# Nearest neighbours and sixteen residual layers on one core: low parts by adding DMAs, and a reordered first stage

## The reference

```python
sq = jnp.sum(xyz * xyz, axis=1)
d2 = sq[:, :, None] + sq[:, None, :] - 2.0 * jnp.einsum('bdn,bdm->bnm', xyz, xyz)
_, idx = jax.lax.top_k(-d2, 8)
...
for i in range(4):                          # and the whole again: 8 layers
    shortcut = points
    p = leaky_relu(points)                  # slope 0.01
    g = group_point(p, idx_t)               # p of the 8 nearest points
    c = jnp.einsum('oi,bin->bon', w[i], p)
    gn = jnp.einsum('oi,bikn->bokn', w[i], g)
    points = (c + gn.sum(axis=2)) / 9.0 + shortcut
```

## Time and profile before

| | |
|---|---|
| median of three runs | 345.85 us |
| the profiled execution's own time | 345.5 us |
| its span in the trace | 343.4 us |
| PE busy | 322.1 us (94%) |
| DVE busy | 276.8 us (81%) |
| ACT busy | 164.3 us (48%) |
| POOL busy | 87.8 us (26%) |
| DMA, hardware queue | 18.36 MB, 16.8% of 16 engines |

### The profile page before, as it was taken

One profiled execution on the slowest core, in us unless ns is written; L12 is line 12 of the kernel. 1 busy time (PEld: TensorE's weight loads), 2 busy tenths in 40 slices (PEclk: granted clock), 3 DMA queues, 4 the chain that ended last, 5 costly groups with the idle time before them and its releaser, 6 DMA issues.

```text
span 343.4 us, 5071 instructions
## 1 busy us (share of the span) xinstructions
PE 322.1 (94%) x2024; PEld 293.3 (85%) x2024; DVE 276.8 (81%) x350; ACT 164.3 (48%) x246; POOL 87.8 (26%) x76
## 2 busy tenths in 40 slices
PE   4999799969989869999999999999999999999996
PEld 4999799969979758887888988898898889889884
DVE  3998999999999594888867777977877796787773
ACT  4536445533726714355844655436265643626510
POOL 2000000000006302333724523514252351425200
PEclk9999999989999989999999999999999999999999
DMA  7945534514700000000000000000000000000023
GB/s 242 326 147 168 153 98 143 180 61 124 240 22 1 0 2 0 2 0 0 2 0 2 0 3 2 0 2 0 2 0 2 0 0 2 0 2 0 37 88 122
DMA packets 7311, 18.68 MB, mean 54 GB/s; under 512 B 628, under 2 KB 1908, under 8 KB 7288
## 3 DMA queue, kind: packets, MB, share of 16 engines
q1 hardware_dynamic: 7288, 18.36, 16.8%
HBM read 16.26 MB, written 2.10 MB: 53 GB/s over the span
## 4 chain that ended last, share of the span: by engine, by line
PE 46%; DVE 5%; ACT 1%; issue 1%; DVEq 0%
PE wide L424 26%; PE wide L413 7%; PE wide L400 6%; PE wide L402 6%; DVE r_mixed L658 1%; DVE y_rest L726 1%; DVE y_lo L730 1%; DVE state L738 1%; ACT y_hi L572 1%; ACT relu L564 0%; PE wide L386 0%; DVEq L713 0%; ACT r_high L567 0%; DVEq L729 0%
## 5 line engine op out<-in xcount | busy, mean ns | idle before, releaser
L281 POOL TENSOR_TENSOR r_low<-relu,r_high 128x512 fp32r<-128x512 f32 x64 | 85.5, 1351 | 234.2 <-ACT r_high L567 234.2
L424 PE MATMUL wide<-adj,y_hi 128*128 128x512 f32 (+1 forms) x260 | 101.8, 393 | 0.8 <-DVE state L738 0.8
L424 PE MATMUL wide<-adj,y_lo 128*128 128x512 f32 (+1 forms) x260 | 101.7, 393 | 0.0
L726 DVE TENSOR_TENSOR y_rest<-wide,y_hi 128x1024 f32<-128x1024 f32 x32 | 39.2, 1224 | 43.3 <-ACT y_hi L572 43.3
L400 PE MATMUL wide<-w_high,r_high 128*128 128x256 f32 x256 | 63.6, 286 | 0.4 <-DVE y_rest L726 0.4
L402 PE MATMUL wide<-w_low,r_low 128*128 128x256 f32 x256 | 63.2, 284 | 0.0
L572 ACT CAST y_hi<-wide 128x1024 fp32r<-128x1024 f32 x32 | 32.3, 1008 | 62.4 <-PE wide L402 62.4
L564 ACT ACTIVATE relu<-state 128x512 f32<-128x512 f32 x64 | 40.2, 629 | 39.2 <-DVE state L738 30.4
L424 PEld LDWEIGHTS wide<-adj,y_hi 128*128 128x128 f32 x260 | 48.9, 188 | 11.2 <-DVE state L738 1.2
L424 PEld LDWEIGHTS wide<-adj,y_lo 128*128 128x128 f32 x260 | 49.0, 188 | 10.2
L400 PEld LDWEIGHTS wide<-w_high,r_high 128*128 128x128 f32 x256 | 49.4, 193 | 2.1 <-issue 0.8
(11 more groups left out here) (59 smaller groups left out, 289.5 us busy)
## 6 DMA issues: line engine op xcount, KB each, us to landing
raw<-in_ctx_dram SPq DMA_DIRECT2D x23, 512.0 KB, 4.2
state<-in_x_dram SPq DMA_DIRECT2D x4, 512.0 KB, 6.4
out_dram<-state SPq DMA_DIRECT2D x3, 512.0 KB, 2.8
w_raw<-in_fside_BxSxS_dram SPq DMA_DIRECT2D x1, 1024.0 KB, 10.8
rest_raw<-in_ctx_dram SPq DMA_DIRECT2D x4, 130.0 KB
raw<-in_ctx_dram SPq DMA_DIRECT2D x2, 256.0 KB, 3.2
out_dram<-state SPq DMA_DIRECT2D x1, 256.0 KB, 2.0
out_dram<-state SPq DMA_DIRECT2D x2, 128.0 KB, 1.7
```

The costliest lines, as they stand in the source:

```text
L281: nc.gpsimd.tensor_tensor(r_low[:, n % 3, h, :], relu[:, h, :], r_high[:, n % 3, h, :].bitcast(fp32), ALU.subtract).then_inc(r_low_ready, 1)
L424: mm = nc.tensor.matmul(bank[to][:, cols], part[:, s % 2, q, h * P:(h + 1) * P], adj[:, b, q, cols], start=(q == 0 and part is y_hi), stop ...
L726: nc.vector.tensor_tensor(y_rest[:, :, :], wide[MAIN][:, :].rearrange("p (q o) -> p q o", q=NB), y_hi[:, s % 2, :, :].bitcast(fp32), ALU.s ...
```

## The change

Six edits go together. (1) `BY_DMA` is (1, 3, 5): in batches 1 to 3 the low parts of units 1, 3 and 5 are no longer computed on VectorE. ACT multiplies the loaded words by -`LEAN` in place, and a DMA issued by GpSimd reads the same words from DRAM once more and adds them. (2) A load waits for the main products of the unit one batch earlier (`main_used`) and for its mixed part (`g_mixed_ready`); VectorE's `points_mixed` now waits for `unit_used` itself. (3) The row of half squares is one fp32 product of `ones` and `half_diag`; the split into two fp32r parts is gone. (4) On VectorE `distances` comes after unit 1's mixed and unit 2's low part, the other units are dispersed between the searches, and the four `weights` stand behind unit 0 of batch 1. ACT's order is moved accordingly. (5) `turn_neighbours(2)`, `copy_adj(2)` and the third relu come after the first `y_step`. (6) `ENTER` is 9, and what is done for batch 3 between the steps comes one step later.

```diff
-    BY_DMA = ()
+    BY_DMA = (1, 3, 5)
...
-        ENTER = 8
+        ENTER = 9
...
                     if k < PAIRS:
-                        sp.wait_ge(unit_used, (b - 1) * PAIRS + k + 1)
+                        sp.wait_ge(main_used, (b - 1) * PAIRS + k + 1)
                     else:
-                        sp.wait_ge(mixed_summed, b * NB)
+                        sp.wait_ge(main_summed, b * NB)
+                    sp.wait_ge(g_mixed_ready[k], b)
...
-                pe.wait_ge(diag_split, b + 1)
-                nc.tensor.matmul(bank[SQ_BANK][:, :], ones[:, :], diag_hi[:, :], start=True, stop=False)
-                nc.tensor.matmul(bank[SQ_BANK][:, :], ones[:, :], diag_lo[:, :],
-                                 start=False, stop=True).then_inc(sq_row_ready, 1)
+                pe.wait_ge(diag_ready, b * NB + NB)
+                nc.tensor.matmul(bank[SQ_BANK][:, :], ones[:, :], half_diag[:, :], start=True, stop=True)\
+                    .then_inc(sq_row_ready, 1)
...
                 mixed_products(b, 4)
-                if b == B - 1:
-                    turn_neighbours(B - 2)
...
                 if s == 0:
+                    turn_neighbours(B - 2)
+                if s == 1:
                     square_row(B - 1)
...
-                if s == 1:
+                if s == 2:
                     turn_distances(B - 1)
...
+            points_parts(1, 0)
+            points_parts(1, 1)
             weights_high(0)
             weights_high(1)
-            points_parts(1, 0)
-            points_parts(1, 1)
+            points_parts(1, 2)
+            points_parts(1, 3)
             weights_high(2)
             weights_high(3)
-            points_parts(1, 2)
             copy_main(0)
-            points_parts(1, 3)
+            points_parts(1, 4)
             for b in range(1, B):
-                points_parts(b, 4)
+                points_parts(b, 5)
+                points_parts(b, 6)
                 if b >= 2:
                     copy_adj(b - 2)
-                points_parts(b, 5)
-                points_parts(b, 6)
+                copy_low(b - 1)
...
+                if b > 0 and k < PAIRS:
+                    dve.wait_ge(unit_used, (b - 1) * PAIRS + k + 1)
+                elif b > 0:
+                    dve.wait_ge(mixed_summed, b * NB)
...
                 diagonals(b - 1)
-                split_diagonal(b - 1)
-                for k in (2, 3, 5):
-                    points_low(b, k)
-                    points_mixed(b, k)
+                points_low(b, 1)
+                points_mixed(b, 1)
+                points_low(b, 2)
                 distances(b - 1)
...
+                points_mixed(b, 2)
+                points_low(b, 3)
+                points_low(b, 4)
+                points_mixed(b, 3)
+                points_low(b, 5)
                 neighbours(b - 1, 0)
                 neighbours(b - 1, 1)
+                points_low(b, 6)
+                points_mixed(b, 6)
+                points_mixed(b, 4)
+                neighbours(b - 1, 2)
+                neighbours(b - 1, 3)
+                points_mixed(b, 5)
...
-                if s == 0:
+                if s == 1:
                     distances(B - 1)
                     relu_mixed(2)
...
-                if 2 <= s < 2 + NB:
-                    neighbours(B - 1, s - 2)
-                if s == 6:
+                if 3 <= s < 3 + NB:
+                    neighbours(B - 1, s - 3)
+                if s == 7:
                     add_selves(B - 1)
```

More of the change, by code:

```diff
@@ L100, in knn_blocks_kernel @@
         half_diag = sb("half_diag", [P, N], fp32)
-        diag_hi = sb("diag_hi", [P, N], fp32r)
-        diag_lo = sb("diag_lo", [P, N], fp32r)
         half_sq = sb("half_sq", [P, NB], fp32)
@@ L108, in knn_blocks_kernel @@
         eyes = sb("eyes", [P, NB, P], bf16)
-        ones = sb("ones", [P, P], fp32r)
+        ones = sb("ones", [P, P], fp32)
         w_raw = sb("w_raw", [P, BLOCKS, CH, C], fp32)
@@ L176, in knn_blocks_kernel @@
         unit_in = [sem(f"unit_in_{k}") for k in range(UNITS)]
+        main_used = sem("main_used")
         unit_used = sem("unit_used")
@@ L193, in knn_blocks_kernel @@
         diag_ready = sem("diag_ready")
-        diag_hi_ready = sem("diag_hi_ready")
-        diag_split = sem("diag_split")
         sq_row_ready = sem("sq_row_ready")
@@ L282, in relu_low @@
                                             ALU.subtract).then_inc(r_low_ready, 1)
-            pool.memset(ones[:, :].bitcast(fp32), 1.0).then_inc(consts_ready, 1)
+            pool.memset(ones[:, :], 1.0).then_inc(consts_ready, 1)
             pool.memset(ident[:, :], 0.0).then_inc(eye_zeroed, 1)
@@ L328, in main_products @@
                             mm.then_inc(main_summed, 1)
+                if k < PAIRS:
+                    mm.then_inc(main_used, 1)
             def mixed_products(b, k):
@@ L595, in _ @@
                         nc.scalar.mul(w_low[:, l, :, :], w_raw[:, l, :, :], SHIFT).then_inc(w_ready, 1)
-                copy_low(b - 1)
                 if b < B - 1:
@@ L601, in _ @@
                     points_parts(b + 1, 2)
+                    points_parts(b + 1, 3)
                     copy_main(b)
                     neighbour_marks(b - 1, 1)
-                    points_parts(b + 1, 3)
+                    points_parts(b + 1, 4)
                 else:
@@ L608, in _ @@
                     relu_parts(1)
+                    copy_main(b)
                     neighbour_marks(b - 1, 1)
-                    copy_main(b)
-                    copy_adj(b - 1)
-                    relu_parts(2)
             for s in range(B * LAYERS):
@@ L616, in _ @@
                 y_high(s)
-                if s == 1:
+                if s == 0:
+                    copy_adj(B - 2)
+                    relu_parts(2)
+                if s == 2:
                     copy_low(B - 1)
-                if s == 4:
+                if s == 5:
                     neighbour_marks(B - 1, 0)
-                if s == 6:
+                if s == 7:
                     neighbour_marks(B - 1, 1)
@@ L690, in diagonals @@
                                                    accum_out=half_sq[:, i:i + 1]).then_inc(diag_ready, 1)
[L691 to L697, removed]
             def distances(b):
@@ L743, in _ @@
                 points_mixed(0, k)
-            dve.wait_ge(consts_ready, 2 + NB)
-            weights(0)
-            weights(1)
             points_low(1, 0)
             points_mixed(1, 0)
[L749 to L752, removed]
+            dve.wait_ge(consts_ready, 2 + NB)
+            for l in range(BLOCKS):
+                weights(l)
             for b in range(1, B):
@@ L757, in _ @@
                 diagonals(b - 1)
-                split_diagonal(b - 1)
-                for k in (2, 3, 5):
-                    points_low(b, k)
-                    points_mixed(b, k)
+                points_low(b, 1)
+                points_mixed(b, 1)
+                points_low(b, 2)
                 distances(b - 1)
-                for k in (6, 4):
-                    points_low(b, k)
-                    points_mixed(b, k)
+                points_mixed(b, 2)
[3 more added lines that the diff above has]
+                points_low(b, 5)
                 neighbours(b - 1, 0)
                 neighbours(b - 1, 1)
+                points_low(b, 6)
[4 more added lines that the diff above has]
+                points_mixed(b, 5)
                 if b < B - 1:
@@ L772, in _ @@
                     weights_mixed(2 * b - 1)
[L773 to L777, removed]
                 else:
                     relu_mixed(0)
-                    relu_mixed(1)
-                    add_selves(b - 1)
+            add_selves(B - 2)
             gram_rows(B - 1)
             diagonals(B - 1)
-            split_diagonal(B - 1)
+            relu_mixed(1)
             for s in range(B * LAYERS):
                 split_y(s)
-                if s == 0:
+                if s == 1:
                     distances(B - 1)
```

## The result

The changed kernel takes 336.09 us (median of 4 runs, 334.24 to 336.89) against 345.99 us before (4 runs, 345.56 to 349.67). The ratio is 0.9684 with a 95% interval from 0.9607 to 0.9761: 3.2% faster, where 336 us was forecast. That is the ratio of the means, which the one long run before (349.67 us) pulls down; the medians are 2.9% apart, as forecast.

A forecast was written before the change was run, and what follows sets the result against it. TensorE was taken to bound the steady steps and VectorE the first stage. Span 343.4 - 11.9 + 1.4 + 2.0 - 1.65 + 0.5 = 333.75, plus 2.1 and 0.35, gave 336 us; range 332 to 344 for 8 in 10.

The forecast's parts named there:

- VectorE to TensorE as the bound: First stage, Gram batches: VectorE's work falls from 29.3 to 24.5 us, just below TensorE's 25.3, so TensorE becomes the bound.
- The stalls: First stage: TensorE's waits for distances, the lower clock behind them and 16 moved transposes go, 11.9 us won in sum.
- The squares' row: Three times in the first stage: one fp32 product costs 0.94 us against 0.47 for two fp32r, 1.4 us lost.
- The adds: Adding DMAs, three per batch: 3.3 us of all engines each, between 1.65 and 10.8, taking DMA's share to some 0.85.
- The landing charge: Batches 2 and 3: loads land at 6 us, each us above 5 costs one per batch; 2 us charged, ends 0 and 11.
- the loop that I drew: From unit 5's mixed part through its next load, ACT, adjacency copy, squares' row, distances and searches: 25.3 us, about TensorE's period.
- Stage to ring: From the first stage's end to y_rest(3): 25.3 us in place of 26.95, 1.65 us won.
- the later entry: ENTER = 9: one more step takes 7.15 us in place of 6.66, 0.5 us lost.
- the ring: Steps while batches 0 to 2 go alone: a cycle through the engines makes y_rest come every 7.15 us, not 6.66.
- A: Rival, first stage: adds crowd the DMA engines and loads land late, costing 11.4 us, time 339 to 347; chance 0.27.
- B: Rival, Gram batches: the adds become the bound and the kernel slower, 366 us at 8 us per add; chance 0.07.
- C: Rival, first stage: VectorE stays the bound, batches of 27 to 28 us, half the stalls stay, 340 to 342; chance 0.06.

The follow-up runs named there:

- control: The changed kernel run again with no edit: 337.06 us, 0.977 of the kernel before.
- no_adds: The changed kernel with BY_DMA = (), so VectorE computes the low parts of units 1, 3 and 5 again: 341.03 us, 0.9877 of the kernel before.
- adj_first: The changed kernel with ACT's adjacency copy before the parts of units 5 and 6 in batches 2 and 3: 334.40 us, 0.9672 of the kernel before.
- mixed5_sooner: The changed kernel with VectorE's mixed part of unit 5 before the last two searches: 336.58 us, 0.974 of the kernel before.
- loads_late: The changed kernel with the loads' old wait condition put back: 345.90 us, 1.0006 of the kernel before.
- enter_8: The changed kernel with ENTER = 8 and batch 3's work between the steps one step earlier: 335.53 us, 0.971 of the kernel before.
- both_orders: The changed kernel with ACT's adjacency copy first and its next-step relu split around y_high where that state is three steps old: 327.96 us, 0.9492.
- two_more_reads: The changed kernel with two more plain 512 KB reads into a spare buffer behind each adding DMA: 342.75 us, 0.9914 of the kernel before.

## Why the prediction was right

The mechanism is the one forecast, and the forecast number agrees with the median; its terms do not all agree alike. That it agrees to 0.1 us is luck. The sum gave a span of 333.75, and the median span of the four is 334.3; but to the span I added 2.45 us (2.1, and 0.35 for the median), and these executions took 1.8 more than their spans. The control's median lies 1.1 us above the forecast.

**VectorE to TensorE as the bound.** Forecast 24.5 us of VectorE's work and a batch of 25.8 for TensorE; measured 22.93 busy and 25.51. VectorE's term was too long, by 1.2 of the 1.6 us because I took the whole window of rows 4, which holds seven full mixed parts where a batch has six. Its wait for the squares' row, some 2 us in the forecast, measured 2.22. no_adds shows the reverse step: with 26.4 us of work on VectorE the batch is 28.0. The periods named as signs were 24.7 and twice 26 to 27; they are 24.53, 25.51 and 26.08 in the first profile and 24.47, 26.04 and 29.36 in the control's.

**The stalls.** 11.9 us were to go and 1.4 to come back by the squares' row. The stage got 10.3 shorter with 0.34 of waiting left, so 10.7 without, against 10.5.

**The squares' row.** 0.38 us more than the pair, forecast 0.47, where the ends were 0.24 and 0.94 for the product itself. The Trainium skill's four passes for true fp32 (FP8 and Floating Point Precision, TensorE Precision Notes) give the same 0.94 that I took; from the start of the product to that of the low ones, less 1.18 for the group between, the trace has 0.85, a little under.

**The adds.** 3.3 us of all engines was forecast, 3.07 measured. The Trainium skill's fit for a GpSimd-issued transfer (DMA: Bandwidth & Descriptors, Anatomy of one DMA), an estimated 3.2 us from start to end, does not hold for an add beside other loads: it lands in 6.2 us in one execution of the changed kernel and 7.3 in the other (medians of nine).

**The landing charge, 2 us.** Right in size and place, by a reason that was half right. The profile of the result lost 0.34 us, the control's 3.7 more, some 4.1; adj_first, which takes the wait away, is 2.7 us below the control and 1.7 below the result's median. The median of the result is 1.85 us above its profiled execution, and that is nearly the term: had I compared with the profiled execution alone, my sum of 335.85 would have been 1.6 too long. The charge had nothing for the lower clock behind a wait, which in the control's profile is 1.7 of the 4.1 us. What failed is the loop that I drew: the load's start after VectorE's last piece is not what rules (mixed5_sooner), and the sooner start matters most for unit 3 (loads_late). I had written that loads start 3.5 us sooner and given it no value; it is worth 8.8 us with the adds in place. So the sum holds these sooner loads only unsaid, inside the terms in which every part is there in time.

**Stage to ring, and ENTER.** T + 25.3 forecast (T is the stage's end), 25.55 measured; 0.5 lost by the later entry forecast, 0.7 measured in the spans and 1.0 by enter_8. I had written that the ring exists only while batches 0 to 2 go round alone, and that TensorE bounds the steady steps at 6.66 us. Both are a little wrong: every third steady step has the same ring, and without it a step takes 6.59 us (both_orders). The forecast did not suffer, since the change touches neither.

**Rivals.** A happened in part, in some executions. B did not: an add would have had to cost 6.5 us. C did not. The range was 332 to 344; the median lies inside.

## What to carry to other kernels

Handing work from a full engine to DMA pays where its landing has slack, and costs where something urgent stands behind it in an in-order queue: the same adds were worth 4 us with the new order and sooner loads, and cost 16 with the old ones. A late load hurts through what is queued behind it, so put the copy that TensorE waits for ahead of work that depends on a load; here TensorE's wait is gone in all three profiles that have this order. And a steady stage with TensorE "busy" for 99.9% can still hide a wait: compare the lengths of equal groups in the chain.

## What the runs showed of the hardware

An fp32 product of 128x128 by 512 columns costs 0.85 us of TensorE, about 3.5 times an fp32r one (0.24), and the records show only 0.46 of it before the next start. An accumulating DMA of 512 KB takes 3.07 us of 16 engines, twice a plain one, and keeps GpSimd for 0.86 us. TensorE's products behind a wait of 2.01 us ran at the lower clock (2.99 us for eight that take 1.74 otherwise); behind one of 0.34 us they did not (1.73). The length of the wait alone does not decide it: behind 1.83 us in mixed5_sooner the eight took 3.08, behind 2.41 us in two_more_reads 1.74, and in the kernel before the eight behind a wait of 2.67 us took 1.43 and those behind 3.08 us 2.39. No run here shows what does. The same 512 KB load, unit 5's for batch 3, took 5.7, 7.3 and 8.3 us from issue to landing in three profiles.
